# A fused attention and quantised-linear kernel: the token transfer ahead of the maxima in SyncE's list, and GpSimd's linear work in other blocks

## The reference

```
xn  = (x - mean) / sqrt(var + 1e-5)
q   = xn @ Wq.T   (16 heads of 16);  k, v = xn @ Wk.T, xn @ Wv.T   (8 heads of 16, each used by 2 query heads)
att = softmax((q k.T - |i - j| * slope_head) / 4) @ v,   then att @ Wo.T + bo
s   = max(max|xn|, 1e-6) / 127 per token;  xq = clip(round(xn / s), -128, 127)
lin = (xq @ weight_q.T) * s * weight_scale + bias
out = x + att + lin
```

## Time and profile before

| | before |
|---|---|
| runs, us | 1604.26, 1603.3, 1603.0; median 1603.3 |
| profiled execution, us | 1604.17, of which the span is 1602.4 |
| TensorE busy | 1567.9 us, 98% |
| VectorE busy | 1429.5 us, 89% |
| ScalarE busy | 1220.8 us, 76% |
| GpSimd busy | 1066.9 us, 67% |
| granted TensorE clock | 0.997 of full |

### The profile page before, as it was taken

How to read it: one execution, slowest core, us unless ns; L and a number is a source line. 1 busy time by engine, 2 the same in 40 slices (tenths; PEclk the granted TensorE clock), 3 DMA queues, 4 the chain that set the end, 5 groups by cost and what they waited for, 6 DMA issues and landing times.

```text
span 1602.4 us, 53471 instructions
## 1 busy us (share of the span) xinstructions
PE 1567.9 (98%) x22012; PEld 785.0 (49%) x22012; DVE 1429.5 (89%) x1666; ACT 1220.8 (76%) x2394; POOL 1066.9 (67%) x1595
## 2 busy tenths in 40 slices
PE   5899999999999999999999999999999999999998
PEld 4344444545545545545545545545545545444443
DVE  6999999999999999999999999999999998999981
ACT  4477777777787787787787787787787787888875
POOL 5577787787777777777777777777777776333332
PEclk9999999999999999999999999999999999999999
DMA  8222222232232232223233223223223222111111
GB/s 195 71 69 59 72 75 62 77 79 79 81 79 80 82 78 80 82 75 83 81 77 81 82 73 85 82 75 83 81 73 85 79 67 62 52 52 50 45 46 54
DMA packets 182215, 121.03 MB, mean 76 GB/s; under 512 B 99988, under 2 KB 154644, under 8 KB 181972
## 3 DMA queue, kind: packets, MB, share of 16 engines
q1 hardware_dynamic: 181972, 117.62, 27.4%
HBM read 81.40 MB, written 35.63 MB: 73 GB/s over the span
## 4 chain that ended last, share of the span: by engine, by line
PE 83%; DVE 7%; SPq 4%; issue 3%; DMA 2%; POOL 1%; ACT 1%; DVEq 0%; POOLq 0%; ACTq 0%
PE ps_pv L1227 25%; PE ps_ring L1163 24%; PE ps_row L1163 24%; DVE row_max L885 4%; PE ps_ring L1259 3%; SPq L417 3%; PE ps_ring L1278 3%; DMA token_b<-token_dram 2%; PE ps_ring L1262 1%; PE ps_ring L1272 1%; DVE xn L812 1%; PE ps_row L1251 1%; DVE stats L802 1%; ACT probs L1048 1%; PE ps_ring L1178 0%
## 5 line engine op out<-in xcount | busy, mean ns | idle before, releaser
L885 DVE TENSOR_REDUCE row_max<-ps_row 128x1 f32<-128x1024 f32 x1024 | 1204.5, 1215 | 109.4 <-PE ps_row L1163 108.5
L1048 ACT ACTIVATE probs<-ps_ring 128x512 f32<-128x512 f32 x2048 | 1114.0, 600 | 216.1 <-PE ps_ring L1163 165.2
L1163 PE MATMUL ps_ring<-q,k 122*32 122x512 bf16 x8192 | 727.9, 379 | 1.7 <-ACT probs L1048 1.0
L1163 PE MATMUL ps_row<-k,q 120*32 120x512 bf16 x8192 | 635.7, 380 | 10.8 <-issue 4.9
L674 POOL TENSOR_TENSOR probs<-probs,near 128x256 f32<-128x256 f32 x512 | 380.8, 744 | 301.9 <-ACT probs L1048 255.9
L1227 PE MATMUL ps_pv<-probs,v_unit 128*32 128x512 f32 x4096 | 537.4, 593 | 5.5 <-POOL probs L674 5.5
L1163 PEld LDWEIGHTS ps_row<-k,q 120*32 120x32 bf16 x8192 | 240.4, 97 | 327.1 <-issue 159.5
L1163 PEld LDWEIGHTS ps_ring<-q,k 122*32 122x32 bf16 x8192 | 232.3, 95 | 318.4 <-issue 129.4
L1227 PEld LDWEIGHTS ps_pv<-probs,v_unit 128*32 128x32 f32 x4096 | 130.9, 110 | 81.6 <-POOL probs L674 10.9
L697 POOL TENSOR_TENSOR xt_step<-xt,token_b 128x256 f32<-128x256 f32 x53 | 45.8, 863 | 66.2 <-PE ps_ring L1163 46.0
L1259 PEld LDWEIGHTS ps_ring<-xn_t,wqk 128*128 128x128 f32 x636 | 78.7, 192 | 2.4
(11 more groups left out here) (85 smaller groups left out, 916.2 us busy)
## 6 DMA issues: line engine op xcount, KB each, us to landing
parts_dram<-parts SPq DMA_DIRECT2D x59, 288.0 KB, 3.3
token_b<-token_dram SPq DMA_DIRECT2D x53, 256.0 KB, 3.4
q<-parts_dram SPq DMA_DIRECT2D x128, 96.0 KB
q<-parts_dram SPq DMA_DIRECT2D x128, 64.0 KB
att_dram<-att_unit SPq DMA_DIRECT2D x126, 64.0 KB
att_t<-att_dram SPq DMA_DIRECT2D x56, 128.0 KB, 2.9
out<-out_tile SPq DMA_DIRECT2D x55, 128.0 KB, 2.9
xt<-x_t SPq DMA_DIRECT2D x53, 128.0 KB, 3.1
```

Source lines behind the costliest of these rows:

```text
L885: dve.tensor_reduce(row_max[:, par, e, qb:qb + 1], ps_row[qb % 2][:, :], AX_X, ALU.max, negate=True).then_inc(row_max_found, 1)
L1048: act.activation(probs[:, c % PBUFS, e, h * HALF:(h + 1) * HALF], ring_bank(u, c, e, h), ACT.Exp, scale=SCALE).then_inc(ring_freed, 1)
L1163: mm = pe.matmul(to[at, :], weights[:, at], moving, start=start, stop=stop)
```

## The change

On SyncE `load_token(u+12)` moves from behind `place_max` and `load_set` to ahead of `place_max`. On GpSimd `weigh_linear` keeps its multiplication alone, which moves to chunk 4, and the two additions are a function `add_weighted` of their own in chunk 5. `add_first_linear` is divided in the same manner: `weigh_first_linear` stands in chunk 3 and the additions in chunk 7, ahead of `finish`. No instruction is added or removed. Lines behind the changed ones move by two to five: L674 is L676 in the changed kernel, L722 is L724, L648 is L650, L745 is L747, L758 is L762.

```diff
@@ SyncE, unit(u, f) @@
+                if f["normed"]:
+                    load_token(u + 1 + PREP_AHEAD)
                 if not f["last"]:
                     place_max(u + 1, (u + 1) % SETS)
                 if f["row_set"]:
...
                     load_set(u + 3, (u + 3) % SETS)
-                if f["normed"]:
-                    load_token(u + 1 + PREP_AHEAD)
@@ GpSimd @@
-            def add_first_linear(t):
+            def weigh_first_linear(t):
                 here = lin_first[:, t, :]
                 pool.wait_ge(first_lin_ready, t + 1)
                 pool.tensor_tensor(here, here, wscale[:, :], ALU.mult).then_inc(
                     first_lin_weighted, 1)
+
+            def add_first_linear(t):
                 pool.wait_ge(first_lin_weighted, t + 1)
-                add_linear(t, here, first_base_ready, t)
+                add_linear(t, lin_first[:, t, :], first_base_ready, t)
...
                                    ALU.mult).then_inc(lin_weighted, 1)
+
+            def add_weighted(t):
                 pool.wait_ge(lin_weighted, t - PREP_AHEAD + 1)
                 add_linear(t, lin[:, t % 2, :], base_ready, t - PREP_AHEAD)
...
+                    if c == 4 and f["made"]:
+                        weigh_linear(t - 1)
                     if c == 5 and f["made"]:
-                        weigh_linear(t - 1)
+                        add_weighted(t - 1)
...
-                    if c == 6 and u < PREP_AHEAD:
+                    if c == 3 and u < PREP_AHEAD:
+                        weigh_first_linear(u)
+                    if c == 7 and u < PREP_AHEAD:
                         add_first_linear(u)
```

## The result

| | before | changed |
|---|---|---|
| median of 4 runs, us | 1603.15 | 1592.12 |
| lowest to highest | 1601.17 to 1604.26 | 1591.08 to 1592.71 |
| profiled execution, us | 1604.17 | 1592.4 |
| its span, us | 1602.4 | 1590.6 |

The ratio is 0.9932, with a 95% interval of 0.9915 to 0.9949: 11.0 us less, where 1592.1 us had been forecast.

What follows compares the result with a forecast made beforehand. TensorE, with 83% of the chain of waits, was taken to bound the kernel. Gains of 3.6 + 2.3 + 5.3 = 11.2 us off 1603.3 gave 1592.1, range 1590.5 to 1594.5 (chance 0.66).

Steps and rivals of the forecast that it cites:

- The floor and the places: TensorE's list, 23.99 us a full unit; time added at the ends of the first eleven units and by token numbers.
- The token load: SyncE's earlier load ends GpSimd's late work beside VectorE's chain: 3.6 us of 3.9 in units 11 to 52.
- The first linear part: GpSimd, first eleven tiles: dividing it makes the weighing of chunk 7 0.2 to 0.5 us late instead of 3.2.
- Units 9 to 11: Three steps from unit 8 to 11 fall to the floor of 23.99: 74.3 - 72.0 = 2.3 us.
- Units 1 to 8: VectorE's chain limits them to about 23.45 us each: 192.9 becomes 187.6, a gain of 5.3, bounds 2.5 and 7.9.
- TensorE's own list: Floor of units 1 to 8, without the projection's matmuls: 23.12 us each, allowing 7.9 us if VectorE doesn't limit.
- The 0.87: Us by which units 1 to 8, without the projection's four matmuls, were taken to be shorter than a full unit.
- VectorE's limit: Its rival: VectorE doesn't limit units 1 to 8, gain 7.9 there, 13.8 in all, 1589.5 us; chance 0.08.
- The splitting of q and k: Rival: GpSimd's earlier cast and subtraction fall beside VectorE's scale and statistics in units 1 to 8, 3.3 us lost, 1595.4; chance 0.08.
- The token was the cause: Its rival: the token isn't the cause of late units from 12 on, only 7.6 us remain, 1595.7; chance 0.10.
- The maxima: Rival: on the DMA queue they land late behind the token's packets, each of 51 units pays, 1618 at 0.5; chance 0.04.

Runs made afterwards that it cites:

- run 1: Kernel before with only the token load moved ahead of the maxima: 1597.46 us, ratio 0.9965.
- run 6: Changed kernel with `shift_turned` behind the weighing of chunk 1 instead of chunk 0: 1597.95 us, ratio 0.9966.
- run 2: Changed kernel with `load_token` back behind `load_set`, so only GpSimd's order differs from the kernel before: 1599.94 us, ratio 0.9977.
- run 3: Changed kernel with the `weigh_linear` multiplication (L747) back in chunk 5, only the first tiles' part divided: 1592.25 us, ratio 0.9932.
- run 4: Changed kernel with VectorE's transposition back (`turn_back`) moved from chunk 1 to chunk 2 in units 1 to 8: 1589.48 us, ratio 0.9914.
- run 9: Changed kernel with `turn_back` in chunk 2 and the statistics in chunk 4, in units 0 to 8: 1590.14 us, ratio 0.9911.
- run 7: Changed kernel with the token load held until the maxima are kept, issued directly ahead of them: 1591.47 us, ratio 0.9926.

## Why the prediction was right

**The floor and the places.** Right. Units 9 to 52 take 23.99 us now, with one exception (below).

**The token load.** Forecast 3.6 us of the 3.9 in units 11 to 52, measured 987.4 - 983.8 = 3.6. The remainder is unit 21, which takes 24.27 in all kernels of this study. The mechanism, that the late token costs time through VectorE's chain and not through a wait for GpSimd's result, is shown by runs 1 and 6. The prediction named `normalise` (L812) alone, and that is only 0.41 of the 0.94 by which unit 31's chain was longer. The other 0.53 is the instruction ahead of it, L931, here in unit 31 beside L702 and in unit 29 without it:

```profile
822.52 0.86 POOL L702 TENSOR_TENSOR xn_t<-xt_step,token_b 128x256 f32<-128x256 f32 x1
822.72 0.95 DVE L931 TENSOR_TENSOR att_normed<-pv_turned,rsum 128x256 f32<-128x256 f32 x1
```

```profile
774.74 0.42 DVE L931 TENSOR_TENSOR att_normed<-pv_turned,rsum 128x256 f32<-128x256 f32 x1
```

This matters because one of the two alone stays within the slack. In the trace of the kernel before, of units 12 to 50, the 13 in which both were long hold 3.5 us of the excess, and the 17 in which one was long cost at most 0.03 each (unit 21 left out in both, see the end). All of these units follow one rule within 0.02 us, and so do those of runs 2 and 6: 23.99 as long as the way from L915 (L923) to the reduction behind the chain takes up to 4.96, and above that each microsecond is paid in full. 5.05 gives 24.09, 5.37 gives 24.40 and 5.54 gives 24.57. With 4.42 to 4.43 for an undisturbed chain this is the slack of 0.53 to 0.55.

The issue came at 293.06, 4.1 us after the token store, and 3.3 ahead of the maxima, as worked out.

**The first linear part.** Right in time and nearly in detail. The weighing of chunk 7 is 0.5 us late instead of 3.2, at the upper end of the 0.2 to 0.5 given. The weighing of chunk 0 behind `finish` is 0.8 late in unit 10, not at most 0.5; it had no price. That moving the other multiplication is worth nothing was forecast and run 3 shows it.

**Units 9 to 11.** Forecast 2.3, measured 74.3 - 72.0 = 2.3.

**Units 1 to 8.** Forecast 23.44 a unit and 5.3 us, measured 187.7 / 8 = 23.46 and 5.2. The step that mattered was to ask which wait is next: TensorE's own list would have allowed 7.9 by the forecast, and 7.4 by runs 4 and 9. Run 4 shows that it was VectorE's chain, run 6 the slack of 0.55 that a full unit has. TensorE's own list without the projection was put at 23.12; runs 4 and 9 end at 23.20 and 23.18, so that bound was 0.06 to 0.08 too low. The 0.87 had been read from starts in tenths of a microsecond; unrounded, the same steps are 24.75 and 23.93, which gives 0.82 and 23.17. The forecast didn't suffer, since 23.99 - 0.87 + (0.87 - 0.55) is 23.99 less the slack, whatever the 0.87 is.

**The rivals.** VectorE's limit exists (runs 4, 6). The splitting of q and k fell beside VectorE's statistics without effect: unit 4's chain from L923 to the reduction is 4.42 us, as in unit 29 of the earlier trace rows. The token was the cause (run 1). The maxima land 0.5 us later directly behind the token's packets, and TensorE doesn't notice (run 7).

What the prediction did not say is that its two parts need each other in units 1 to 8, where 1.9 us of the 5.2 are in neither part alone, in these executions (run 2's expectation had it, once the chain was known as the limit).

## What to carry to other kernels

A late transfer need not delay the engine that waits for it to cost time: here GpSimd had time to spare, but its work, started late, fell beside VectorE's and lengthened that. So look at what a delayed block of work will run beside, and not only at who waits for its result. A loss that stays within the slack shows nothing in the time, and two small ones in the same unit do. And before a wait is counted as gained, measure the slack of the next one: in units 1 to 8 it decided 2.1 of 7.4 us, and a half-microsecond transposition moved one chunk later gave that back. Small work between paced instructions is free in small pieces only; one microsecond in one place cost more than it saved, and half of it in each of two places did not.

## What the runs showed of the hardware

- A VectorE f32 TENSOR_SCALAR of 128x256 (L812, L820) takes 0.41 us alone. When it starts while a GpSimd TENSOR_TENSOR of the same size is under way, it ends 0.15 to 0.16 us after GpSimd's, however far into it it started (0.15 to 0.40 us), and so takes 0.81 to 0.83 (before, beside L674) or 0.94 to 0.97 (runs 2 and 6, beside L704).
- A VectorE TENSOR_TENSOR of 128x256 with both inputs in SBUF (L931) takes 0.42 alone. In all 39 cases of the trace before in which it was longer, up to 0.99, it ended 0.28 to 0.29 us after a GpSimd instruction that was under way when it started.
- GpSimd's weighing takes 0.73 and its L704 0.86. In the traces before and of runs 2 and 6 they took 0.90 to 0.99 and 0.94 to 1.14, and only where they started while L931 (L939) ran, or together with it. An L931 that started later didn't lengthen them (22 weighings of the trace before). So between these instructions the one that started first went through, and the other was held until it ended.
- VectorE's reductions and transpositions from PSUM kept their times beside the same GpSimd work: L915 takes 0.71 beside L702, as elsewhere.
- Unit 21 takes 0.27 us more than its neighbours in every trace, whatever the kernel. It isn't the late token, as it is there in runs 1 and 7 too. The time is lost at the end of the unit, here in the changed kernel, with the same matmul of unit 20 behind it:

```profile
582.78 1.57 ACT L1056 ACTIVATE probs<-ps_ring 128x512 f32<-128x512 f32 x3 [0.39 <-PE ps_ring L1171]
...
583.43 0.09 PEld L1186 LDWEIGHTS ps_ring<-eye_b,neg_max 128*32 128x32 bf16 x1 [0.67 <-ACT probs L1056]
```

```profile
559.17 0.09 PEld L1186 LDWEIGHTS ps_ring<-eye_b,neg_max 128*32 128x32 bf16 x1 [0.38 <-ACT probs L1056]
```

ScalarE starts the second exponent of chunk 4 0.27 later than in unit 20, in all twelve traces (at 580 to 591 us), and TensorE waits for it. Why ScalarE is late there no run shows.
